# One block for the token phase and the first experts, which run in two passes

## The reference

```python
logits = x_flat @ W_router                      # 16384 tokens, 8 experts
probs = jax.nn.softmax(logits, axis=-1)
topk_p, topk_i = jax.lax.top_k(probs, 2)
topk_p = topk_p / topk_p.sum(axis=-1, keepdims=True)
combine = (jax.nn.one_hot(topk_i, E) * topk_p[..., None]).sum(axis=1)
for e in range(E):
    h = jax.nn.relu(x_flat @ W1[e] + b1[e])     # 128 -> 512
    y = h @ W2[e] + b2[e]                       # 512 -> 128
    out = out + combine[:, e:e + 1] * y
```

## Time and profile before

| | us |
|---|---|
| median of three runs | 1269.37 (1269.09 to 1271.05) |
| profiled execution, its own time | 1271.14 |
| its span | 1269.3 |
| TensorE busy | 1077.3 (85%) |
| VectorE busy | 911.5 (72%) |
| ScalarE busy | 797.3 (63%) |
| GpSimd busy | 550.3 (43%) |
| first and last dispatch start | 195.1, 370.6 |
| first and last expert result start | 393.2, 816.3 |

### The profile page before, as it was taken

How to read it: one execution, slowest core, us unless ns; L and a number is a source line. 1 busy time by engine, 2 the same in 40 slices (tenths; PEclk the granted TensorE clock), 3 DMA queues, 4 the chain that set the end, 5 groups by cost and what they waited for, 6 DMA issues and landing times. The chain is left out here.

```text
span 1269.3 us, 34850 instructions
## 1 busy us (share of the span) xinstructions
PE 1077.3 (85%) x9969; PEld 731.1 (58%) x9970; DVE 911.5 (72%) x2119; ACT 797.3 (63%) x2044; POOL 550.3 (43%) x402
## 2 busy tenths in 40 slices
PE   6869979988209999999999999668999999965698
PEld 2324435554109999999999999623334433422464
DVE  2662348767826888888878878628999999983587
ACT  5865569998405777777777777546566665622465
POOL 0000006757752333333333333327999999991000
PEclk9989989999558999999999999869999999985599
DMA  6200001451431111111111111130112221102000
GB/s 195 80 1 0 0 1 43 133 173 53 91 56 45 45 42 46 41 44 42 43 45 43 43 44 43 34 92 17 34 49 66 66 66 36 48 34 84 0 2 34
DMA packets 60527, 65.25 MB, mean 51 GB/s; under 512 B 9841, under 2 KB 50301, under 8 KB 60336
## 3 DMA queue, kind: packets, MB, share of 16 engines
q1 hardware_dynamic: 49616, 46.47, 12.9%
q0 software_dynamic: 8832, 17.00, 4.2%
q10 hardware_dynamic: 2016, 0.94, 0.6%
HBM read 37.12 MB, written 28.55 MB: 52 GB/s over the span
## 5 line engine op out<-in xcount | busy, mean ns | idle before, releaser
L933 ACT ACTIVATE m_hh<-ps 128x256 f16<-128x256 f32 x584 | 224.3, 384 | 118.2 <-PE ps L890 88.6
L833 POOL DMA_INDIRECT expert_out<-m_result,m_token x148 | 145.5, 983 | 305.3 <-DVE m_result L989 299.2
L970 DVE SCALAR_TENSOR_TENSOR m_hl<-ps,m_hh 128x256 f16<-128x256 f32 x584 | 241.6, 422 | 44.4 <-ACT m_hh L933 35.3
L870 PE MATMUL ps<-m_x,weights 128*128 128x128 f16 x1168 | 212.9, 220 | 3.5 <-DVE m_hl L970 2.6
L871 PE MATMUL ps<-m_x,weights 128*128 128x128 f16 x1168 | 212.8, 220 | 0.0
L874 PE MATMUL ps<-m_x,weights 128*128 128x128 f16 x1168 | 212.8, 220 | 0.0
L888 PE MATMUL ps<-weights,m_hh 128*128 128x128 f16 x1160 | 210.0, 219 | 0.0
L889 PE MATMUL ps<-weights,m_hh 128*128 128x128 f16 x1160 | 209.9, 219 | 0.0
L890 PE MATMUL ps<-weights,m_hl 128*128 128x128 f16 x1160 | 209.9, 219 | 0.0
L776 POOL DMA_INDIRECT dispatched<-d_rows,slot x128 | 130.2, 1017 | 154.3 <-DVE slot L684 108.0
L1098 POOL TENSOR_TENSOR iv_pool_sum<-iv_pool_sum,iv_pool_part 128x1024 f32<-128x1024 f32 x80 | 188.7, 2359 | 11.7 <-DVE iv_pool_part L1313 3.8
(11 more groups left out here) (305 smaller groups left out, 2299.9 us busy)
## 6 DMA issues: line engine op xcount, KB each, us to landing
m_rows<-dispatched SPq DMA_DIRECT2D x152, 65.5 KB, 1.8
X<-x SPq DMA_DIRECT2D x16, 512.0 KB, 4.4
iv_got<-expert_out SPq DMA_DIRECT2D x16, 512.0 KB, 4.3
out<-X SPq DMA_DIRECT2D x16, 512.0 KB, 3.1
Y<-w_moe SPq DMA_DIRECT2D x8, 512.0 KB
expert_out<-m_result,m_token POOLq DMA_INDIRECT x148, 2.3
dispatched<-d_rows,slot POOLq DMA_INDIRECT x128, 2.6
Y<-w_last SPq DMA_DIRECT2D x1, 2048.0 KB
```

The source lines that it names most:

```text
L833: pool.indirect_dma_start(env.yt, bass.IndirectOffsetOnAxis(ap=token[:, k:k + 1], axis=0), result[:, k, :], None, bounds_check=TOKENS - 1, ...
L870: pe.matmul(out, high, xh, start=True, stop=False)
L933: act.activation(hh[e][:, part_cols[h]], hidden[e][h], ACT.Relu).then_inc(hi_ready[e], 1)
L970: dve.scalar_tensor_tensor(hl[e][:, cols], hidden[e][h], 0.0, hh[e][:, cols], ALU.max, ALU.subtract).then_inc(h_split[e], 1)
```

## The change

The two phases become one block. `experts0` returns five programs, one for each engine, which the token phase's programs call at their ends; its buffers lie in columns of `Y` that held `w_last`. Every engine but VectorE first waits for the semaphore `tables`, which VectorE raises when the row table is there.

The experts run in two passes over the 28 pairs, 56 entries in all. The first pass takes the full tiles of each pair among the tokens of units 0 to 23 (spans 0 to 7; at least one tile for each pair, and where a pair has no full one, a tile of padding), the second pass takes all the rest. SyncE waits for the dispatches of spans 0 to 7 ahead of its first row load and for all dispatches and the padding before the group in which the second pass begins. The padding is written by SyncE alone, 28 transfers between its row loads of the second group of eight tiles.

The weights move into the token loop: `w_last` is loaded first (after unit 4), the experts' weights after it one by one, each after the one before has landed; subtraction for expert e in unit 8 + 2e; rounding in units 9, 11, 13, 15, 19, 23, 27, 29; VectorE's low parts one unit later; the first half of the bias work in unit 30, the second half before the last `route`. There are eight result buffers instead of four, all of them free at the start, and the stores come in groups of eight.

```diff
-RING, OUTS = 8, 4
-ROW_TABLE = 160
+RING, OUTS, LANDINGS = 8, 8, 4
+ROW_TABLE = 200
...
+EARLY = 7
+BASE_AT = {8 + 2 * e: e for e in range(E0)}
+ROUND_AT = {n: e for e, n in enumerate((9, 11, 13, 15, 19, 23, 27, 29))}
+BIAS_AT = 30
...
+    def experts_sync(sp):
+        def group(j, pads):
+            def announce(k):
+                sp.wait_ge(landed[k % (RING // 2)], j * 32 + (16 if k < RING // 2 else 32))
+                sp.sem_inc(rows_ready, 1)
+
+            for k in range(RING):
+                i = j * RING + k
+                row = sp.value_load(env.row_table[0:1, bass.ds(i, 1)], min_val=0, max_val=(PAIRS + 1) * REGION - SLOT)
+                sp.wait_ge(out_ready, i + 1)
+                sp.dma_start(rows[:, k, :], env.xg[bass.ds(row, SLOT), :]).then_inc(landed[k % (RING // 2)], 16)
+                if k > 0:
+                    announce(k - 1)
+                for p in pads[k]:
+                    pad(sp, p)
+            announce(RING - 1)
+
+        sp.wait_ge(tables, 1)
+        groups = count(sp, 1, ENTRIES // RING, ROW_TABLE // RING)
+        early = count(sp, 3, PAIRS // RING, MAX_TILES // RING)
+        early_rows(sp)
+        group(0, [[]] * RING)
+        group(1, [[p for p in range(PAIRS) if p * RING // PAIRS == k] for k in range(RING)])
+        with sp.Fori(2, early) as j:
+            group(j, [[]] * RING)
+        all_rows(sp)
+        with sp.Fori(early, groups) as j:
+            group(j, [[]] * RING)
+
+    def experts_gpsimd(pool):
+        pool.wait_ge(tables, 1)
+        pool.sem_inc(result_free, OUTS)
...
+            if k >= 2:
+                pool.wait_ge(stored[(k - 2) % LANDINGS], j * (16 * OUTS // LANDINGS) + 16 * ((k - 2) // LANDINGS + 1))
+                pool.sem_inc(result_free, 1)
...
+        for entry in range(ENTRIES):
+            pair, following = PAIR_LIST[entry % PAIRS], PAIR_LIST[min(entry + 1, ENTRIES - 1) % PAIRS]
+            if entry % 2 == 0:
+                word = pe.value_load(env.words[0:1, entry // 2:entry // 2 + 1], min_val=0, max_val=FIELD ** 3 - 1)
...
+        def early_rows(sp):
+            for k in range(SENT_SETS):
+                sp.wait_ge(sent[k], sum(tiles_in(c) for c in range(k, EARLY + 1, SENT_SETS)) * 16)
...
+            sp.wait_ge(sum_ready, E0 * H0 // HALF)
+            sp.dma_start(last_row, a["w1_last"]).then_inc(w_loaded, 16)
             for e in range(E0):
-                sp.wait_ge(sum_ready, E0 * 2 + e)
+                sp.wait_ge(sum_ready, E0 * H0 // HALF + (e + 1) * 2 * H0 // HALF)
+                sp.wait_ge(w_loaded, 16 * (e + 1))
                 sp.dma_start(raw[:, e, :], a["w_moe0"][e, :, :]).then_inc(w_loaded, 16)
...
                 normalize(n)
-            act.wait_ge(w_loaded, 16 * (E0 + 2))
-            for e in range(2):
-                round_weights(e)
+                if n in ROUND_AT:
+                    round_weights(ROUND_AT[n])
             shares(SPANS - 1)
-            for e in range(2, E0):
-                round_weights(e)
-            pad(act, 1)
+            experts.scalar(act)
...
+                if n in BASE_AT:
+                    base(BASE_AT[n])
+                if n - 1 in ROUND_AT:
+                    low_weights(ROUND_AT[n - 1])
+                if n == BIAS_AT:
+                    bias_parts()
             scores(UNITS - 1)
             choose(SPANS - 1)
             pair(SPANS - 1)
             share(SPANS - 1)
+            bias_rows()
             route(SPANS - 1)
...
+            dve.tensor_scalar(tiles[:, first_pass], seen_early[:, :], float(SLOT), None, ALU.max)
+            link(dve.tensor_scalar(tiles[:, second_pass], seen[:, :], float(SLOT - 1), float(SLOT), ALU.add, ALU.max))
+            link(dve.tensor_copy(whole, tiles))
+            link(dve.tensor_scalar(whole, whole, SLOT.bit_length() - 1, None, ALU.arith_shift_right))
+            link(dve.tensor_copy(tiles, whole))
+            link(dve.scalar_tensor_tensor(full[:, :], seen_early[:, :], float(SLOT), tiles[:, first_pass], ALU.is_ge, ALU.mult))
+            link(dve.tensor_tensor(tiles[:, second_pass], tiles[:, second_pass], full[:, :], ALU.subtract))
+            link(dve.tensor_scalar(tiles[:, second_pass], tiles[:, second_pass], 1.0, None, ALU.max))
...
+            dve.tensor_copy(env.row_table[:, :], turned[0][0:1, 0:ROW_TABLE]).then_inc(tables, 1)
+            experts.vector(dve)
```

More of the change, by code:

```diff
@@ L4 @@
+from collections import namedtuple
 from contextlib import ExitStack, contextmanager
@@ L405, in phase_tokens0 @@
         hot = sb("r0_hot", [P, SPAN, PAIRS], BF16)
-        seen, fresh = sb("r0_seen", [P, PAIRS]), sb("r0_fresh", [P, PAIRS])
+        seen, seen_early, full = sb("r0_seen", [P, PAIRS]), sb("r0_seen_early", [P, PAIRS]), sb("r0_full", [P, PAIRS])
         v = {k: sb(f"r0_{k}", [P, SPAN])[:, :] for k in
              ("top1", "top2", "rev1", "rev2", "gap", "ex", "g1", "g2", "swap", "hi", "lo", "pid", "rank")}
[L409 to L415, removed]
+        spent = [k[:, :, :].rearrange("p t e -> p (t e)") for k in (l, hit, l2)]
+        start, tiles, cumt, delta = (spent[i][:, k * ENTRIES:(k + 1) * ENTRIES] for i, k in ((0, 0), (0, 1), (1, 0), (2, 0)))
+        whole = spent[2][:, ENTRIES:2 * ENTRIES].bitcast(I32)
+        words, ends = spent[1][0:1, ENTRIES:ENTRIES + ENTRIES // 2], sb("r0_ends", [1, PAIRS], I32)
+        last_row = Y[:, 0:E0 * H0]
+        raw = Y[:, E0 * H0:E0 * 3 * H0].rearrange("p (e n) -> p e n", e=E0)
         rest0 = E0 * 3 * H0
@@ L459, in step_at, with all_rows, pad @@
             return done[0] if done and done[0] < SPANS - 1 else None
[L461 to L466, removed]
+        def early_rows(sp):
+            for k in range(SENT_SETS):
+                sp.wait_ge(sent[k], sum(tiles_in(c) for c in range(k, EARLY + 1, SENT_SETS)) * 16)
+        def all_rows(sp):
+            for k in range(SENT_SETS):
+                sp.wait_ge(sent[k], sum(tiles_in(c) for c in range(k, SPANS, SENT_SETS)) * 16)
+            sp.wait_ge(padded[0], 16 + 16 * (PAIRS // 2))
+            sp.wait_ge(padded[1], 16 * (PAIRS // 2))
+        def pad(sp, p):
+            if p == 0:
+                sp.wait_ge(ends_ready, 1)
+            end = sp.value_load(ends[0:1, p:p + 1], min_val=(p + 1) * REGION, max_val=(p + 2) * REGION - SLOT)
+            sp.dma_start(env.xg[bass.ds(end, SLOT), :], env.zero[:, :]).then_inc(padded[p % 2], 16)
+        experts = experts0(nc, env, ctx, tables, low, early_rows, all_rows, pad)
         @block.sync
@@ L534, in _ @@
             mm.then_inc(counted, 1)
+            experts.tensor(pe)
         @block.scalar
@@ L997, in phase_involution @@
+            experts.gpsimd(pool)
 def phase_involution(nc, env, a, out):
```

462 lines of the change are left out of this document (221 added, 241 removed).

## The result

The changed kernel takes 1258.77 us (median of four runs, 1257.66 to 1259.91), the kernel before 1269.23 (1269.00 to 1271.05) on the same chip: ratio 0.9915, 95% interval 0.9897 to 0.9932. A second series gave 1260.55 against 1268.88, ratio 0.9921 (0.9900 to 0.9941). The forecast was 1260.4.

A forecast was written before the change was run, and what follows sets the result against it. TensorE bounds the expert stage, but idled nearly 50 us before it, with GpSimd's dispatch ending last. Terms -26.1 + 5.2 + 5.2 + 6.7 = -9.0 gave 1262.1, or 1260.4 us in the median's terms; range 1251.5 to 1269.5.

The forecast's parts named there:

- Token loop, +7.3: Token loop: eight weight roundings of 1.04 us move onto ScalarE, one hidden behind a wait for TensorE, adding 7.3 us.
- VectorE covered, +0.65: Token loop: VectorE's pauses hide its added low parts, subtractions and bias work, except about 0.65 us at the last unit.
- slower rival: Token loop: VectorE's added 18.5 us are not covered and lie on the chain, giving 1278.3 us; chance 0.10.
- Bias rows +1.6, tables +1.4: After the loop: 4.1 us of bias work in VectorE's 2.50 us wait adds 1.6; longer tables add 1.4.
- First product forecast at 356.2: Start of experts: first product waits for VectorE's tables, not the last dispatch; at 356.2 instead of 382.26, -26.1 us.
- Clock at the start: First expert tiles: TensorE's clock is at its lower level after some 15 us without work, so they stay as slow.
- Word loads +5.2: Expert stage: 14 more loads of words of bounds by TensorE, 0.37 us each, at entries of even pairs, add 5.2 us.
- Empty stores +5.2: End of experts: eight buffers give seven empty stores instead of three, four more at 1.29 us, adding 5.2 us.
- Padding +6.7: Expert stage: 28 pads at 1.15 us on SyncE make TensorE wait at tiles 12 to 15, adding 6.7 us.
- Padding hidden: Rival, expert stage: pads issue faster, under 0.91 us each, so TensorE does not wait; 1253.7 us, chance 0.17.
- Entries dearer: Rival, expert stage: each new entry costs TensorE 0.37 us even without a word load; 1265.6 us, chance 0.15.
- gains and losses cancel: Rival: pads at 1.25 us, clock falling in the pauses (+3), loop losing another 3 to VectorE; 1269 us, chance 0.10.

The follow-up runs named there:

- e6: Changed kernel with the weights' rounding moved from ScalarE to VectorE, in the units where the low parts are taken: 1267.05 us, ratio 0.9977 to the kernel before.
- e7: Changed kernel with the first half of the bias work in unit 26, its last subtraction and another operation in 28: 1260.18 us.
- e4: Changed kernel with SyncE waiting for the dispatch of all ten spans ahead of the first row load: 1282.64 us, ratio 1.0104 to the kernel before.
- e8: Changed kernel with the word of the next two entries loaded ahead of the last tile of the entry before: 1255.19 us.
- e3: Changed kernel with each of TensorE's 28 words of bounds loaded twice: 1277.85 us, ratio 1.0077 to the kernel before.
- e2: Changed kernel with four result buffers instead of eight and stores in groups of four: 1255.19 us, ratio 0.9896 to the kernel before.
- e1: Changed kernel with the 28 pads written between the row loads of two groups of eight tiles instead of one: 1250.89 us.
- e5: The changed kernel itself run again, nothing altered: 1260.55 us, ratio 0.9921 to the kernel before.
- e10: Changed kernel with VectorE rounding, roundings and low parts in lighter units, bias work in four pieces: 1239.08 us, with 143 tiles instead of 145.
- e12: Changed kernel with pads over two groups, word one tile early, four result buffers, VectorE rounding in light units, split bias work (first copy in unit 26): 1240.42 us.
- e11: Changed kernel with pads over two groups, word one tile early, VectorE rounding in light units, split bias work, eight buffers: 1224.63 us, with 143 tiles.

## Why the prediction was right

- **Number of tiles: right.** 145 results in both traces.
- **Token loop, +7.3: right.** +6.7, seven roundings of 1.04 and small changes of the waits at the choices.
- **VectorE covered, +0.65: right as a sum, but nearer the edge than I had it.** Route starts at 339.38, 8.9 later than before when unit 0 is taken as the mark; the forecast terms up to there are 7.3 + 0.65 + 1.6 = 9.6. The slower rival (VectorE uncovered, 1278.3) did not happen, but its mechanism is real: 7.2 us more of work in the wrong units cost 7.6 in e6, with the clock's falls in it, and the bias work moved in e7 brought nothing.
- **Bias rows +1.6, tables +1.4: right.** 335.26 to 339.35 is the forecast 4.1; from L999 to the row table's product 7.6 us, against 5.95 + 1.4 = 7.4 forecast.
- **First product forecast at 356.2, measured at 354.11.** 2.5 us stem from before unit 0; without them it is 0.4 late. The end of the dispatch came at 372.0 instead of 375.8, of which 2.5 are again the mark. e4, which takes back the early start alone, loses 22 to 24 us: the early start is shown to be the cause of the gain.
- **Clock at the start: wrong, in my favour.** I left the first tiles as slow as before. It rises between 357 and 358, some 3.5 us behind the first product; before it took until 391, 9 us behind 382.26. That makes the -2.0 to the first result; e4, the same program started late, gives them back. The windows after and before:

```profile
356.00:357.00 1.00, 1.00 (x13) 1.00 (x11) 0.64 (x2) 0.50 (x2) 0.83 (x1) 0.50 0.53 134
357.00:358.00 1.00, 0.83 (x8) 0.56 (x6) 0.64 (x2) 0.73 (x3) 0.86 (x1) 0.61 0.51 134
358.00:360.00 2.00, 1.54 (x25) 1.37 (x26) 0.62 (x2) 0.35 (x3) 1.39 (x3) 1.00 0.35 88
```

```profile
390.00:391.00 1.00, 1.00 (x12) 1.00 (x11) 0.00 (x0) 0.35 (x2) 0.00 (x0) 0.50 0.27 67
391.00:392.00 1.00, 1.00 (x19) 1.00 (x17) 0.62 (x2) 0.66 (x2) 0.00 (x0) 0.89 0.31 67
```

- **Word loads +5.2: right**, at the forecast places and size (3.27 a step), and e8 leaves at most 0.15 of each. As the price of a load, 0.37 was wrong (e3).
- **Empty stores +5.2: right** to a tenth, and e2 gives them back.
- **Padding +6.7: right mechanism, size off by 2.** 437.1 - 144 x 2.905 - 27 x 0.37 = 8.8, e1: 8.7. A pad was 1.11 where I took 1.15. The group began 1.9 us later than assumed, because SyncE first announces tile 7 once its row has landed, and one issue took 1.42 instead of 0.35 (0.69 in e5). TensorE's clock, which I had as a bound of +3, cost nothing: it fell once and not at all in e5, with 437.1 and 437.3 from first to last result, because the end of the wait is SyncE's: it announces tile 15 at 406.70, and TensorE, which has waited for it once more, takes it at 406.90.
- **Padding hidden: fell** (1.11 a pad, above the 0.91 that it needed). **Entries dearer: fell.** Odd entries show no excess and e8 leaves at most 0.15 at an even one, while the instruction queue moved twice as much from 350 to 800 us:

```profile
q8 instruction: 52, 0.85, 0.8%
```

The Trainium skill (Runtime: NRT & Kernel Launch, Instruction fetch mechanics) has a taken branch stall when its target lies outside the current two-page window. The 52 fetches for 26 are as many as twice the tile bodies need when each is fetched once, so no jump back made a fetch of its own, as far as the counts tell: these runs do not put that rule to the test, for or against.

- **The other rivals: fell.** The case in which gains and losses cancel (1269) needed pads of 1.25, a clock that costs 3 and 3 more in the loop; none came. The first product did not wait for the dispatch, which ended 18 us later.

The sum of my terms with the measured ones: -28.2 + 2.5 (mark) - 2.0 + 5.2 + 8.8 + 5.2 = -8.5, where the medians have -8.3 and -10.5. The misses at clock and padding, -2.0 and +2.1, cancelled, so that the total is better than its parts is luck.

What stays open: why TensorE's clock falls in one execution and not in another of the same program, which goes with 2 to 3 us in stages that are the same; how e6's loss divides between place and clock; and whether GpSimd could leave the empty stores out one by one, which was not tried.

## What to carry to other kernels

When a wait is taken out of the middle of a chain, price what was parked beside it: here 28 pads, 14 register loads and four empty stores, all cheap, gave back 19 of the 32 us won between the loop and the first product, and each was taken off again, the loads in part, by another place or size alone (two groups, one tile earlier, stores in fours). Before work is moved to an engine with a free share of 16%, look at the units where it is late already: the same roundings cost 7.6 us in one set of units and left a gain of 2.0 to 4.3 in another, with the bias work split (e6; e10 to e12). And a buffer count is right only for the distance between two engines' starts; when that distance changes, it has to be counted anew (e2 and e12).

## What was not expected of the hardware

- A register load on TensorE's queue costs 0.65 us when another load stands ahead of it, 0.37 in the pace when a tile's matmuls do, and at most 0.15 one tile earlier.
- The clock after short pauses of TensorE is not the same in two executions of one program: a pause of 2.3 us inside a busy stretch was followed by 3.4 us at the lower level in one trace of the changed kernel, later pauses were not, and in its second trace none was (1.00 from 388 to 412 us). Loops of the same program with and without such falls took 147.4 and 145.1 us (e11, e10).
- With 11.0 and 5.0 us of waiting in place of 41.2 the clock was up again some 3.5 us behind the first product instead of 9; with 10.9 and 26.9 us (e4) it took 9.3.
- An empty indirect store takes GpSimd 0.98 + 0.30 us, as long as a full one.
- A pad (register load and issue on SyncE) is 1.11 us when SyncE does them alone, 1.25 when two queues issue them, nearly all of the difference in the register load, 0.27 against a median of 0.39; one row load's issue in between took 1.42 instead of 0.35, and 0.69 at the same place in e5.
